# Attention and a routed feed-forward block in f32: all experts on all tokens, or each expert on sorted tiles of its own tokens

## What is computed

```python
x = x + xattn(layernorm(x), ctx, ctx, ...)          # 16 heads of 16
h = layernorm(x)
scores = sigmoid(h @ gate_w.T)                      # 32 experts, in 8 groups of 4
sc = scores + gate_bias                             # 4 best groups by their two best, then the 8 best experts
combine = (one_hot(tki, 32) * tkw[..., None]).sum(1)    # tkw: their scores, normalised, times 2.5
g = silu(einsum('th,eih->tei', h, w_gate)); u = einsum('th,eih->tei', h, w_up)
routed = einsum('tei,ehi->th', g * u * combine[:, :, None], w_down)
shared = silu(h @ sh_gate.T) * (h @ sh_up.T) @ sh_down.T
x = x + routed + shared
```

## Time and profile before

| What | us |
|---|---|
| Median of two runs (lowest, highest) | 689.49 (688.76, 690.22) |
| The profiled execution | 689.38 |
| Its span | 687.6 |
| Projections, to | 50.5 |
| Attention, to | 165.0 |
| Routing, to | 193.9 |
| Experts, first and second half | 247.7 and 246.0 |

### The profile page before, as it was taken

One profiled execution on the slowest core, in us unless ns is written; L12 is line 12 of the kernel. 1 busy time (PEld: TensorE's weight loads), 2 busy tenths in 40 slices (PEclk: granted clock), 3 DMA queues, 4 the chain that ended last, 5 costly groups with the idle time before them and its releaser, 6 DMA issues.

```text
span 687.6 us, 13004 instructions
## 1 busy us (share of the span) xinstructions
PE 625.4 (91%) x4232; PEld 569.0 (83%) x4232; DVE 559.5 (81%) x942; ACT 271.4 (39%) x590; POOL 249.4 (36%) x222
## 2 busy tenths in 40 slices
PE   3897999997589999999999999999999999999996
PEld 3885666664489898999999899999999999999995
DVE  5967999994748888888888888888888888888885
ACT  3444665652123333333333333333333333333331
POOL 6530334344013333333333333333333333333332
PEclk9999999998779999999999999999999999999998
DMA  6210000000123343433334343444343433333341
GB/s 192 80 59 1 2 2 3 2 2 0 49 74 94 98 133 97 122 111 113 120 101 131 95 125 109 131 120 125 102 131 94 130 104 119 115 102 132 95 123 49
DMA packets 33373, 61.66 MB, mean 90 GB/s; under 512 B 4008, under 2 KB 14768, under 8 KB 33348
## 3 DMA queue, kind: packets, MB, share of 16 engines
q1 hardware_dynamic: 33348, 61.31, 29.6%
HBM read 59.44 MB, written 1.86 MB: 89 GB/s over the span
## 4 chain that ended last, share of the span: by engine, by line
PE 76%; DVE 16%; issue 5%; ACT 1%; DMA 1%; POOL 0%; SPq 0%; DVEq 0%
PE ps L647 47%; PE ps L813 24%; DVE prob L498 4%; DVE rden L519 3%; DVE nm L489 2%; PE ps L834 2%; DVE st L509 1%; DVE xn L445 1%; DMA cst<-consts 1%; DVE ot L521 1%; DVE x_all L507 1%; PE ps L737 1%; PE ps L700 0%; PE ps L710 0%; PE ps L696 0%
## 5 line engine op out<-in xcount | busy, mean ns | idle before, releaser
L302 POOL TENSOR_TENSOR act<-act,cw 128x400 f32<-128x400 f32 x136 | 178.8, 1315 | 328.5 <-DVE act L595 328.5
L647 PE MATMUL ps<-h_hi_all,w_hi 128*128 128x400 f32 x544 | 189.0, 347 | 4.9 <-DVE w_lo L544 4.9
L393 ACT ACTIVATE act<-ps 128x400 f32<-128x400 f32 x136 | 68.5, 504 | 311.6 <-PE ps L647 311.6
L647 PE MATMUL ps<-h_lo_all,w_hi 128*128 128x400 f32 x544 | 188.9, 347 | 0.0
L647 PE MATMUL ps<-h_hi_all,w_lo 128*128 128x400 f32 x544 | 188.6, 347 | 0.0
L592 DVE SCALAR_TENSOR_TENSOR act<-act,ps 128x400 f32<-128x400 f32 x136 | 77.7, 571 | 83.5 <-ACT act L393 83.5
L813 PE MATMUL ps<-a_hi,w_hi 128*128 128x400 f32 x272 | 99.2, 365 | 19.5 <-issue 17.0
L647 PEld LDWEIGHTS ps<-h_hi_all,w_hi 128*128 128x128 f32 x544 | 103.2, 190 | 5.0 <-issue 5.0
L647 PEld LDWEIGHTS ps<-h_lo_all,w_hi 128*128 128x128 f32 x544 | 103.3, 190 | 0.0
L647 PEld LDWEIGHTS ps<-h_hi_all,w_lo 128*128 128x128 f32 x544 | 103.2, 190 | 0.0
L544 DVE TENSOR_TENSOR w_lo<-w_raw,w_hi 128x512 fp32r<-128x512 f32 x68 | 102.9, 1513 | 0.0
(11 more groups left out here) (118 smaller groups left out, 664.7 us busy)
## 6 DMA issues: line engine op xcount, KB each, us to landing
cw<-combine_rows SPq DMA_DIRECT2D x68, 400.0 KB, 4.0
w_raw<-w_exp SPq DMA_DIRECT2D x68, 256.0 KB, 3.9
w_raw<-w_exp SPq DMA_DIRECT2D x68, 128.0 KB, 2.0
x_all<-x SPq DMA_DIRECT2D x4, 400.0 KB
ctx_f<-ctx_t SPq DMA_DIRECT2D x4, 400.0 KB, 3.7
out_t<-y_out SPq DMA_DIRECT2D x8, 200.0 KB, 2.0
wa<-w_attn SPq DMA_DIRECT2D x4, 256.0 KB, 6.1
cst<-consts SPq DMA_DIRECT2D x1, 266.0 KB, 5.7
```

The costliest lines, as they stand in the source:

```text
L302: pool.tensor_tensor(act[:, s, :], act[:, s, :], cw[:, (s // 2) % 2, (s % 2) * TG:(s % 2 + 1) * TG], ALU.mult).then_inc(weighted, 1)
L393: a.activation(act[:, s, :], ps[:, 4 + 2 * (s % 2), 0:TG], ACT.Tanh, scale=0.5).then_inc(tanh_e, 1)
L647: last = t.matmul(out, w, m, start=(i == 0), stop=(i == n - 1))
```

## The change

Each expert is applied only to the tokens that chose it. Routing (`route`), the position of each token within its expert (`positions`, small matmuls with a triangular matrix) and its place in device memory (`destinations`) are computed for two batches at a time between the instructions of the attention, from the batch with index 6 on. GpSimd then scatters each normalised row, with its token number and its 32 weights, to its eight experts' regions of a buffer `slots` (`rows_to_experts`, eight indirect DMAs of 100 rows per batch). From the counts a table of 132 tiles of 128 rows is made; this is the most that 12,800 chosen rows can need, and all 132 are always computed. SyncE writes 128 dummy rows behind each expert's last row (32 writes), then loads a tile's rows and weights (`tile_loads`), with addresses that it reads from the table by `value_load` (TENSOR_LOAD in the listings). All 32 experts' weights lie in SBUF, loaded during the attention. A tile is transposed, multiplied in plain f32 with gate and up weights, gated and weighted, transposed and multiplied with the down weights; GpSimd adds the 128 results by indirect DMA to one of two sums in device memory (the first starts as x, the second as zero), alternately, each add waiting for the one two tiles back. At the end both sums are read, transposed and added, and the shared expert's output, computed on TensorE behind the attention, is added on VectorE. The combine weights' detour, the halves and the f32r splits of the experts are gone.

Core of the diff (lines of the two kernels that the text speaks of, eight leading blanks taken off):

```diff
+ID = D
+WT = D + 1
+ROW = D + 1 + NE
+CAP = T + P
+DUMMY = NE * CAP
+SINK = T
+TILES = 132
+RING = 12
+ROUNDS = TILES // RING
+LEVELS = T // P + 1
+XR = 8
+YR = 4
+NS = 2 * NG
+NP = NB // 2
...
+    slots = nc.dram_tensor("slots", (DUMMY + P, ROW), F32).ap()
+    sums = [nc.dram_tensor(f"sums{i}", (SINK + P, D), F32).ap() for i in range(2)]
...
-            wait_alone(sp, gu_lo, E - 1, half_ready, 1)
-            gate_up_load(e + slot, slot)
-            wait_alone(sp, dn_lo, E - 1, half_ready, 1)
-            down_load(e + slot, slot)
-            wait_alone(sp, weighted, CPH * (E - 1), half_ready, 1)
-            combine_loads(h, e + slot, slot)
...
-            pool.wait_ge(cw_in[(s // 2) % 2], 16 * E)
-        pool.wait_ge(gated, N + 1)
-        pool.tensor_tensor(act[:, s, :], act[:, s, :], cw[:, (s // 2) % 2, (s % 2) * TG:(s % 2 + 1) * TG],
-                           ALU.mult).then_inc(weighted, 1)
...
+    for g, (first, end) in enumerate(((6, 11), (11, 17), (17, 23), (23, 30))):
+        sp.wait_ge(pv_psum, BG * (g + 1))
+        experts_load(first, end)
+        sp.wait_ge(x1_ready, BG * (g + 1))
+        sp.dma_start(by_token(sums[0][g * TG:(g + 1) * TG, :]), x_all[:, g * BG:(g + 1) * BG, :]).then_inc(x1_out, 16)
...
+    sp.wait_ge(pad_ready, 1)
+    for b in range(XR):
+        sp.wait_ge(rows_out[b], 16 * TOPK * (NB // XR))
+    for e in range(NE):
+        at = sp.value_load(pad_at[0:1, e:e + 1], min_val=e * CAP, max_val=e * CAP + T)
+        sp.dma_start(slots[bass.ds(at, P), :], pad[:]).then_inc(pads_out, 16)
+    sp.wait_ge(pads_out, 16 * NE)
+    sp.wait_ge(pad_out0, 16)
+    sp.wait_ge(table_ready, 2)
+    def tile_loads(q, s):
+        j = q * RING + s
+        at = sp.value_load(tab[0:1, 1, bass.ds(j, 1)], min_val=0, max_val=DUMMY)
+        e = sp.value_load(tab[0:1, 0, bass.ds(j, 1)], min_val=0, max_val=NE - 1)
+        if not isinstance(q, int):
+            sp.wait_ge(added[s % 2], 16 * ((q - 1) * (RING // 2) + s // 2 + 1))
+        sp.dma_start(tin[:, s, :], slots[bass.ds(at, P), 0:ID + 1]).then_inc(row_in[s], 16)
+        sp.dma_start(wcol[:, s:s + 1], slots[bass.ds(at, P), bass.ds(e + WT, 1)],
+                     allow_slow_non_contiguous=True).then_inc(row_in[s], 16)
...
+    def second_norm(B):
+        if B >= XR:
+            pool.wait_ge(rows_out[B % XR], 16 * TOPK * (B // XR))
+        pool.iota(xr[:, B % XR, ID:ID + 1].bitcast(I32), [[1, 1]], base=B * S, channel_multiplier=1).then_inc(id_ready, 1)
+        pool.wait_ge(var2_ready, B + 1)
+        pool.tensor_tensor(rstd2[:, B % 4:B % 4 + 1], ve2[:, B % 4:B % 4 + 1], minus_half[:, 0:1], ALU.pow).then_inc(rstd2_ready, 1)
+        pool.wait_ge(rstd2_ready, B + 1)
+        pool.tensor_scalar(xr[:, B % XR, 0:D], x_all[:, B, :], mv2[:, B % 4, 0:1], rstd2[:, B % 4:B % 4 + 1],
+                           ALU.subtract, ALU.mult).then_inc(h1_ready, 1)
+    def rows_to_experts(B):
+        pool.wait_ge(dest_ready, B // 2 + 1)
+        for r in range(TOPK):
+            pool.indirect_dma_start(slots[:], bass.IndirectOffsetOnAxis(ap=dest[:, B % XR, r:r + 1], axis=0),
+                                    xr[:, B % XR, :], None).then_inc(rows_out[B % XR], 16)
...
+    for B in range(NB):
+        second_norm(B)
+        if B >= 5:
+            rows_to_experts(B - 5)
...
+    pool.wait_ge(zero_out, 16 * 3)
+    pool.wait_ge(x1_out, 16 * NG)
+    for j in range(TILES):
+        pool.wait_ge(yt_ready, j + 1)
+        if j >= 2:
+            pool.wait_ge(added[j % 2], 16 * (j // 2))
+        pool.indirect_dma_start(sums[j % 2][:], bass.IndirectOffsetOnAxis(ap=tin[:, j % RING, ID:ID + 1].bitcast(U32), axis=0),
+                                ysb[:, j % YR, :], None, compute_op=ALU.add).then_inc(added[j % 2], 16)
...
+    def rows_done(j, q, s):
+        a.wait_ge(yt_psum, j + 1)
+        if not (isinstance(j, int) and j < YR):
+            a.wait_ge(added[s % 2], 16 * (q * (RING // 2) + s // 2 - 1))
+        a.activation(ysb[:, s % YR, :], ps[:, 6 + s % 2, 0:D], ACT.Copy).then_inc(yt_ready, 1)
...
+        then(v.scalar_tensor_tensor(by_group(R(3)), gs[:, 2, :].unsqueeze(2).to_broadcast([S, 2 * NGRP, EPG]), TAKEN,
+                                    by_group(R(2)), ALU.is_equal, ALU.mult))
...
+        v.tensor_scalar(mask_m[:].rearrange("p b e -> p (b e)"), R(4), TAKEN, None, ALU.is_equal).then_inc(mask_ready, 1)
+        then(v.scalar_tensor_tensor(R(3), R(4), TAKEN, R(1), ALU.is_equal, ALU.mult))
...
+    def positions_read(p):
+        if p == 0:
+            v.wait_ge(tables_ready, 7)
+        v.wait_ge(pos_psum, p + 1)
+        by_batch = lambda ap: ap.rearrange("p (b e) -> p b e", e=NE)
+        v.tensor_tensor(by_batch(rt[:, 5, :]), by_batch(ps[0:S, 6, TG:TG + 2 * NE]), ebase[:], ALU.add).then_inc(pos_ready, 1)
...
+    def destinations(p):
+        slot = 2 * p % XR
+        v.wait_ge(pos_ready, p + 1)
+        then(v.scalar_tensor_tensor(rt[:, 0, :], rt[:, 4, :], TAKEN, rt[:, 5, :], ALU.is_equal, ALU.mult))
+        then(*[v.max(best_d[:, b, :], rt[:, 0, b * NE:(b + 1) * NE]) for b in range(2)])
+        v.wait_ge(weights_ready, p + 1)
+        v.tensor_scalar(dest[:, slot:slot + 2, :], best_d[:], -1.0, None, ALU.add).then_inc(dest_ready, 1)
...
+    for i in range(NB):
+        maximum(i)
+        differences(i)
+        if i >= 2:
+            residual(i - 2)
+        if i >= 6 and i % 2 == 0:
+            route(i // 2 - 3)
+        if i >= 1:
+            v.wait_ge(pv_psum, i)
+            if i >= 7 and i % 2 == 1:
+                positions_read((i - 7) // 2)
+            outputs_scaled(i - 1)
+        if i >= 7 and i % 2 == 1:
+            destinations((i - 7) // 2)
...
+    def gate(j, s):
+        v.wait_ge(tanh_e, j + 1)
+        v.scalar_tensor_tensor(opened_t[:, 2 + s % 2, :], opened_t[:, s % 2, :], 1.0, ps[:, 2 + s % 2, 0:FI], ALU.add,
+                               ALU.mult).then_inc(opened, 1)
+        v.wait_ge(opened, j + 1)
+        if not (isinstance(j, int) and j < 2):
+            v.wait_ge(at_psum, j - 1)
+        v.scalar_tensor_tensor(act_t[:, s % 2, :], opened_t[:, 2 + s % 2, :], wcol[:, s:s + 1], ps[:, 2 + s % 2, FI:2 * FI],
+                               ALU.mult, ALU.mult).then_inc(gated, 1)
...
-        if not (isinstance(N, int) and N < 2):
-            t.wait_ge(gated, N - 1)
-        for part_of in range(2):
-            w = lambda a, k: a[:, slot, (2 * part_of + k) * P:(2 * part_of + k + 1) * P]
-            last = product(ps[:, 4 + 2 * (s % 2) + part_of, 0:TG],
-                           [(w(w_hi, k), w(w_lo, k), h_hi_all[:, k, col:col + TG], h_lo_all[:, k, col:col + TG])
-                            for k in range(KC)])
...
-        for m in range(KC):
-            w = lambda a: a[:, slot, 2 * D + m * P:2 * D + (m + 1) * P]
-            for i, (ww, mm) in enumerate(((w_hi, a_hi), (w_hi, a_lo), (w_lo, a_hi))):
-                last = t.matmul(ps[:, (s % 2) * KC + m, 0:TG], w(ww), mm[:, s, :], start=False, stop=False,
-                                skip_group_check=True)
-        last.then_inc(down_done, 1)
...
+    def turn_tile(q, s, j):
+        if not (isinstance(j, int) and j < 2):
+            t.wait_ge(lt_ready, j - 1)
+        t.wait_ge(row_in[s], 32 * (q + 1))
+        for k in range(KC):
+            last = t.transpose(ps[:, s % 2, k * P:(k + 1) * P], tin[:, s, k * P:(k + 1) * P], ident)
...
+    expert = lambda j: t.value_load(tab[0:1, 0, bass.ds(j, 1)], min_val=0, max_val=NE - 1)
+    def gate_up(j, s, e):
+        t.wait_ge(lt_ready, j + 1)
+        if not (isinstance(j, int) and j < 2):
+            t.wait_ge(gated, j - 1)
+        w = w_all[:, bass.ds(e, 1), 0:2 * D].rearrange("p o (t k n) -> p k (o t) n", t=2, k=KC)
+        for k in range(KC):
+            last = t.matmul(ps[:, 2 + s % 2, 0:2 * FI].rearrange("p (t n) -> p t n", t=2), hts[:, s % 2, k, :], w[:, k],
+                            start=(k == 0), stop=(k == KC - 1))
+        last.then_inc(gu_psum, 1)
...
+    def down(j, s, e):
+        t.wait_ge(at_ready, j + 1)
+        if not (isinstance(j, int) and j < 2):
+            t.wait_ge(yt_ready, j - 1)
+        t.matmul(ps[:, 6 + s % 2, 0:D], ats[:, s % 2, :], w_all[:, bass.ds(e, 1), 2 * D:].rearrange("p o n -> p (o n)"),
+                 start=True, stop=True).then_inc(yt_psum, 1)
...
+        for s in range(RING):
+            j = q * RING + s
+            es[s] = expert(j)
+            gate_up(j, s, es[s])
+            if not (last and s + 2 >= RING):
+                turn_tile(q + (s + 2) // RING, (s + 2) % RING, j + 2)
+            if not (first and s < 1):
+                turn_act(j - 1, s - 1)
+            if not (first and s < 2):
+                down(j - 2, s - 2, es[s - 2] if s >= 2 else expert(j - 2))
...
+    for g in range(NG):
+        t.wait_ge(fin_in[g % 2], 32 * (g // 2 + 1))
+        for m in range(KC):
+            if g >= 2:
+                t.wait_ge(y_ready, KC * (g - 2) + m + 1)
+            for j in range(BG):
+                for i in range(2):
```

(3 more changed lines are left out.)

815 lines of the change are left out of this document (454 added, 361 removed).

## The result

The changed kernel takes 742.5 us (median of two runs, 738.0 and 746.9), before 689.5: a ratio of 1.077 with a 95% interval of 1.049 to 1.105. It is slower; forecast were 647 us and "faster". The profiled execution is the one of 746.91 us, with a span of 745.1, so 1.8 us lie around the span, as before.

What follows compares the result with a forecast made beforehand. TensorE bounds the old expert loop, VectorE the attention. First destinations 113.9, last scatter landed 253, paddings to 293.5, first tile 299.5, tiles 323.4, end 22: span 645, plus 1.8 around it, 647 us; range 555 to 765.

Steps and rivals of the forecast that it cites:

- First destinations at 113.9: Attention: six batches at 7.16 us and two at 10.2 bring the first scatter destinations to 113.9 us.
- VectorE's routing per pair: Attention: VectorE's small routing, position and destination instructions add 6.1 us per pair of batches.
- An indirect scatter costs 0.9 us: GpSimd's queue: 128 scatters at 0.9 us, 115 us, and ten norms, 22 us; the last leaves at 251 us.
- rival 4: GpSimd's queue: a scatter costs 1.5 us, VectorE and GpSimd disturbing each other; 724 us, sign turns at 1.23; chance 0.11.
- VectorE sets the attention's pace: Attention with routing: VectorE needs 10.2 us per batch, GpSimd 9.4; VectorE's last destinations come near 226 us.
- TensorE "lies beside it": Attention: TensorE's added work (logits, positions) is small and covered by VectorE's; no time added.
- Paddings, 1.2 us each: SyncE after all scatters: 32 writes at 0.70 for address and issue plus 0.5 for register load, 38 us.
- Tiles, 2.45 us by SyncE: Tile loop: SyncE's two register addresses, two register loads and a wait set the pace; 132 tiles take 323 us.
- rival 1: Tile loop and paddings: register loads are cheap, TensorE and adds set 2.0 us per tile; 577 us; chance 0.26.
- rival 3: Tile loop, GpSimd's wait for the add two tiles back: slow read-modify-write, 3.45 us a tile; 779 us; chance 0.10.
- The end, 22 us: After the tiles: 4 us add landing, 4 us first sums, closing matmuls 14.2 us (2 beside loads), 2 us store.
- Rival 5: Tile loop: TensorE's clock stays at 1.2 GHz, 3.6 us a tile; 799 us; chance 0.03.

## Why the prediction was wrong

**First destinations at 113.9.** Nearly right: 110.85. VectorE's routing per pair too: it is busy for 18.5 us a pair, before for 12.9 (2 x 103.3/16), so 5.6 for 6.1.

**An indirect scatter costs 0.9 us.** This step failed. It was bounded by 0.56 and 2.84 and put between the two smaller rows, because 100 rows of one descriptor each seemed small work. It costs 1.30: 0.99 of the record and 0.30 of issue before the next, whether it carries 100 rows or 50. 128 x 0.4 = 51 us on GpSimd's queue. That is just past the turning point of 1.23 that rival 4 had named, with a chance of 0.11.

**VectorE sets the attention's pace, and TensorE "lies beside it".** This step failed with it; the sum has no term for it. The pair was forecast at 20.4 us and took 28.1, on TensorE: 21.0 us of matmuls per pair at a granted clock of 0.72 (0.97 in attention before), and 6.3 us of holes that no run without real scatters has. So the last destinations came at 261.6 instead of the forecast 226, and GpSimd waited 14.0 us for destinations.

**What each is worth.** On GpSimd's queue the stretch is 63 us longer: 49 of its own time (51 of scatters, a little less of norms) and 14 of waits. The two cover each other, though. An estimate from the timeline: with scatters of 0.9 and the destinations as late as they were, the last three pairs' 48 scatters could start at 246.7 and end at 290; with scatters of 1.30 and no wait for destinations the end is 310.5 - 14.0 = 296.5. Either alone gives back 14 to 21 us, both together the 60 to the forecast 251. That half the scatters gave back 63 us agrees, since that run took away both.

**But not for rival 4's reason.** It blamed VectorE beside GpSimd. In this stretch behind the attention VectorE (third busy time) is nearly idle,

```profile
263.00:310.50 47.50, 15.92 (x29) 6.89 (x28) 3.96 (x9) 0.50 (x1) 36.53 (x37) 0.57 0.32 91
```

and 36.5 us for 37 scatters are the same 0.99 each as in the attention, where VectorE is 62% busy (79.56 of 129.20). The rule of the Trainium skill (SBUF — State Buffer, SBUF: two separate sides) that VectorE can keep GpSimd from writing descriptors changes nothing here by these rows.

**Paddings, 1.2 us each.** Nearly right: 1.10 us (316.07 to 350.24 in 31 steps). That the whole term came out at 43.0 for 42.5 is in part luck: the first padding left 5.5 us after the last scatter's end, where 2 were forecast. Less the 0.70 of a register address, a register load is 0.4 us, near the 0.5 taken. The Trainium skill (DMA: Bandwidth & Descriptors, Latency and other measured facts) has some 600 ns at least; the trace disagrees, 0.4.

**Tiles, 2.45 us by SyncE.** Right in mechanism and nearly in size, 2.58. SyncE's first twelve came 2.24 apart (353.52 to 355.80 to 358.03), those of the loop 2.5; taking one load and one issue away let the next limit show. The limits behind were mis-sized: the adding took GpSimd 1.55, not 0.9, so the chain of adds stood at 2.45, not 1.95, and TensorE at 2.1 (274.8/132), not 1.8. The landing of the add, taken as 3 us, was near (at most 3.35). So rival 1's 2.0 us per tile could not have been reached by cheaper loads, and rival 3's place, at a smaller price, was the bound behind the one that I had. Of the 23 us that this row is longer, 14 are the pace; nearly 8 went at the start, where the first add came 13.6 us after the first load and 6 had been forecast, and the rest is the last add's own time.

**The end, 22 us.** Mechanism right, clock wrong: 14.2 us of closing matmuls were taken at full clock and ran at 0.50, 27.6 us. Rival 5 put this same loss at the tiles, where the clock was 0.97; it came where TensorE idled, 13.5 us before the closing matmuls (701.0 to 714.5). In the stretch of the scatters the clock was 0.71 too. There TensorE is on the chain, so a full clock should shorten the pair, by up to 3.4 us, until GpSimd's own 24.7 is reached; that is an estimate and was not tried.

**The range** held the time (555 to 765), the sign was wrong: the stretch of the scatters alone moved the sum by more than the whole forecast gain of 42 us, through a price multiplied by 128, whose turning point of 1.23 lay well inside its bounds of 0.56 and 2.84, and through an engine that was said to lie beside the pace.

## What to carry to other kernels

An operation that the trace does not show, multiplied by a hundred or more on one queue, decides the sign; where its turning point lies within its bounds, that is no small chance. Before calling an engine the limit, follow the chain back from one of its waits: GpSimd's queue was the longest here, and yet TensorE set the pace while the attention ran. A substitute instruction proves something only if it leaves the other engines as they were. An indirect transfer cost the same with 50, 100 and 128 rows here, so count it per instruction: fill its partitions, and bring down the number of instructions. Where several limits stand close (here 2.58, 2.45 and 2.2 us per tile), removing one gains only the distance to the next, so size all of them: one load per tile alone brought 14 us, with three sums 50.
